# Logits and values from one matmul, and six groups of the result turned by VectorE instead of TensorE

## Chip, core and metric

The kernel runs on one NeuronCore of one Trainium2 chip. The metric is the time of one execution on the device in microseconds (us), as the median of several runs. The slots, groups and phases below are the kernel's own words for pieces of its schedule.

## What is computed

The input `z` has 4 batches of 1024 tokens with 128 features. It is normalised over the features (`xn`). One branch normalises again with a weight and a bias, projects to queries, keys and values of 16 heads with 8 features each, does softmax attention over 1024 keys per batch, projects back and adds `xn`. The other branch is a mixture of 8 experts, of which each token uses its two best. The two are multiplied and added to the input.

```python
xn = _layernorm(x)
zn = (z - mu) / jnp.sqrt(var + 1e-05) * ln_w + ln_b        # z is xn here
qkv = (zn @ W_qkv + b_qkv).reshape(b, n, 3, H, DH)
attn = jax.nn.softmax(einsum('bhqd,bhkd->bhqk', q, k) * scale)
s = xn + (attn @ v) @ W_proj + b_proj
logits = xf @ Wr + br                                      # xf is xn, 8 columns
# softmax over the two largest logits of each token
h = gelu(einsum('td,edh->eth', xf, W1) + b1)
g = silu(einsum('etd,te->td', einsum('eth,ehd->etd', h, W2) + b2, weights))
return x + s * g
```

## The kernel before, in words

The 4096 tokens are 8 groups (`g`) of 512. The kernel has an expert part and an attention part, and each engine's queue is written out by hand with numbered slots.

**Expert part.** Phase `g` has 32 slots for the experts of group `g`. In slot `i` TensorE does `up(i)` (three matmuls, L934 to L936) and `down(i - 3)` (L957, L958, L960, or L952). ScalarE does `gelu(i)` in slot `i` (L812 and L815, or L806). VectorE and GpSimd compute the low halves (`low_h`, L1239 and L670), VectorE also `combine` (L1256) in every fourth slot. The same slots hold the preparation of the next group, `pre(g + 1)`: transposes `t1` and `t2` (L882, L889), the router's logits (L897, 8 columns wide), queries and keys (`qk`, L906 and L907), the turned weights (`w_t`) and the values (`v`, L918: four matmuls of 128 columns). `run_slots` puts in each slot the step of `pre` ahead of that slot's expert step. On ScalarE `z_t` (L766) writes the normalised and turned `znT`, which `qk` and `v` read, and `tanh` (L791) feeds VectorE's `router_weights` (L1189 to L1194).

From slot 36 on, counted over all phases, the queues also hold the early row maxima of the attention scores: a score matmul on TensorE (L974) and a maximum on VectorE (L1321). They use two PSUM banks in turn, so the matmul of maximum `m` waits until maximum `m - 2` has been taken:

```python
EARLY_AT = [HT + 4 + (7 * m) // 10 for m in range(EARLY)]
...
                if m > 1:
                    pe.wait_ge(S("R"), m - 1)
```

That gives one or two of them in each slot. VectorE runs the maximum first in its slot, then the step of `pre`, then `low_h`. Queries and keys are split in three bf16 parts (`rest`, `second`, `third`), stored to DRAM by the SyncE queue, and read back as rows for the maxima (`sp_max_rows`, L433). The rows of head pair 0 need the parts of groups 0 and 1.

**Attention part.** 256 blocks of scores, exponentials (ScalarE, L855, two per block of about 1 us each) and products with the values (L1044). From block 243 on, TensorE's queue also holds the end of the first six groups, one step per block: `project(g)` (L1072) in one block and `y_turn(g)` (L1092, four transposes) in the next. VectorE adds and gates (`sum_y`, `gate_y`) and, after the turn, does `finish` (L1393), which adds the input held in `x_out`. Groups 6 and 7 follow behind the last block. The SyncE queue loads all of `x_out` at the start of the attention part (eight DMAs of 512-byte pieces) and stores it (L580) behind everything that it issues for the blocks.

Every wait of the kernel is on a semaphore with a constant count, in program order on each engine.

## Time and profile before

| | |
|---|---|
| median of 3 runs | 1032.16 us (1031.27 to 1032.86) |
| the profiled execution | 1031.52 us, span 1029.5 us |
| PE busy | 1008.1 us, 98% |
| DVE busy | 842.9 us, 82% |
| ACT busy | 859.4 us, 83% |
| POOL busy | 351.1 us, 34% |
| 16 DMA queues, share of packets | 26.5% |

The span is the part of the execution in which engines work, and what lies around it here is 2 us. The abbreviations: PE is TensorE, DVE VectorE, ACT ScalarE, POOL GpSimd, and SPq is the queue in which SyncE issues DMAs. Busy time of PE includes the pipelined stretch of a matmul, so neighbouring matmuls overlap in it and the distance of their starts is the better price.

### The profile page before, as it was taken

To read this page: it belongs to the slowest core of one execution; us is meant where nothing else is said; L and a number is where in the kernel's file an instruction comes from. 1 tells how busy PE (TensorE), PEld (TensorE's weight loads), DVE (VectorE), ACT (ScalarE), POOL (GpSimd) and SP (SyncE) were. 2 spreads that over 40 slices of the span, in tenths; PEclk is the share of its full clock that TensorE was granted. 3 is DMA by queue.
4 is the path that set the end of the run, shared out by engine and by line. 5 is a ranking of instruction groups with operands and counts; after the bars stand their busy time and mean duration, and the time that the engine had idled before them with its cause. 6 is when DMAs were issued, how large, how long until landed. Compare 5 with 4: busy or idle time off the path is not lost.

```text
span 1029.5 us, 17024 instructions
## 1 busy us (share of the span) xinstructions
PE 1008.1 (98%) x5837; PEld 443.0 (43%) x5869; DVE 842.9 (82%) x1283; ACT 859.4 (83%) x1166; POOL 351.1 (34%) x432
## 2 busy tenths in 40 slices
PE   6999999999999999999999999999999999999998
PEld 4676666666666666667222222222222222222222
DVE  5757878878887887785799999999999999999953
ACT  7877667676767767666999999999999999999985
POOL 5795665656575565746200010001000001000010
PEclk9999999999999999999999999999999999999999
DMA  6542322315132231412421222122221222212113
GB/s 198 131 117 60 103 56 59 102 32 145 31 93 69 57 118 33 113 39 69 116 53 50 55 60 57 42 60 54 54 63 43 58 53 53 59 51 57 26 26 88
DMA packets 102955, 72.11 MB, mean 70 GB/s; under 512 B 25737, under 2 KB 87878, under 8 KB 102870
## 3 DMA queue, kind: packets, MB, share of 16 engines
q1 hardware_dynamic: 102870, 71.04, 26.5%
q8 instruction: 46, 0.75, 0.3%
q14 instruction: 39, 0.32, 0.1%
HBM read 53.12 MB, written 15.59 MB: 67 GB/s over the span
## 4 chain that ended last, share of the span: by engine, by line
PE 87%; DVE 5%; issue 2%; ACT 2%; POOL 0%; another core or an unknown queue 0%; DVEq 0%; ACTq 0%; POOLq 0%
PE psum L1044 22%; PE psum L1004 13%; PE psum L989 10%; PE psum L974 6%; PE psum L934 5%; PE psum L936 5%; PE psum L935 5%; PE psum L952 5%; PE psum L960 4%; PE psum L957 4%; PE psum L958 4%; DVE neg_max_half L1321 1%; DVE neg_max_half L1295 1%; DVE neg_max_half L1291 1%; ACT p_ring L855 1%
## 5 line engine op out<-in xcount | busy, mean ns | idle before, releaser
L855 ACT ACTIVATE p_ring<-psum 128x1024 f32<-128x1024 f32 x512 | 494.5, 1031 | 19.6 <-PE psum L1004 9.1
L1291 DVE TENSOR_REDUCE neg_max_half<-psum 128x2 f32<-128x1024 f32 x240 | 294.3, 1226 | 42.3 <-PE psum L989 34.2
L1044 PE MATMUL psum<-p_ring,v_sb 128*9 128x512 f32 x2048 | 267.6, 594 | 0.2 <-ACT o_sb L846 0.2
L1321 DVE TENSOR_REDUCE neg_max_half<-psum 128x1 f32<-128x512 f32 x304 | 200.0, 685 | 74.9 <-PE psum L974 60.2
L812 ACT ACTIVATE h_hi<-psum,cols 128x512 fp32r<-128x512 f32 x192 | 132.4, 690 | 114.8 <-PE psum L936 114.0
L670 POOL TENSOR_TENSOR h_lo<-h_split,h_hi 128x512 fp32r<-128x512 f32 x128 | 166.2, 1300 | 151.8 <-ACT h_split L815 151.4
L1004 PE MATMUL psum<-q_stack,k_stack 51*128 51x512 bf16 x1024 | 201.2, 385 | 1.3 <-ACT p_ring L855 0.7
L989 PE MATMUL psum<-k_max_stack,q_max_stack 48*128 48x512 bf16 x720 | 182.2, 378 | 1.1
L1004 PEld LDWEIGHTS psum<-q_stack,k_stack 51*128 51x128 bf16 x1024 | 49.1, 92 | 296.6 <-ACT p_ring L855 282.7
L1295 DVE TENSOR_REDUCE neg_max_half<-psum 128x1 f32<-128x512 f32 x240 | 161.2, 672 | 0.0
L624 POOL CAST neg_max_parts<-neg_max_rest 128x16 bf16<-128x16 f32 x32 | 6.5, 203 | 448.4 <-DVE neg_max_rest L1304 448.2
L934 PE MATMUL psum<-xn_t_hi,w_lo 128*128 128x512 f32 x256 | 144.2, 563 | 0.4 <-ACT h_split L815 0.4
L815 ACT ACTIVATE h_split<-psum,cols 128x512 f32<-128x512 f32 x192 | 131.7, 686 | 0.0
L936 PE MATMUL psum<-xn_t_lo,w_hi 128*128 128x512 f32 x256 | 101.6, 397 | 0.0
L935 PE MATMUL psum<-xn_t_hi,w_hi 128*128 128x512 f32 x256 | 101.4, 396 | 0.0
L974 PE MATMUL psum<-k_max_stack,q_max_stack 128*128 128x512 bf16 x272 | 93.3, 385 | 2.6 <-DVE neg_max_half L1321 1.6
L960 PE MATMUL psum<-h_lo,w_hi 128*128 128x512 f32 x192 | 76.1, 396 | 2.2 <-POOL h_lo L670 1.4
L957 PE MATMUL psum<-h_hi,w_lo 128*128 128x512 f32 x192 | 75.7, 394 | 0.0
L958 PE MATMUL psum<-h_hi,w_hi 128*128 128x512 f32 x192 | 74.9, 390 | 0.0
L661 POOL TENSOR_TENSOR acc<-acc,prod 128x512 f32<-128x512 f32 x48 | 64.1, 1336 | 11.7 <-DVE prod L1256 11.7
L952 PE MATMUL psum<-h_full,w_full 128*128 128x512 f32 x128 | 65.4, 592 | 0.0
L1044 PEld LDWEIGHTS psum<-p_ring,v_sb 128*9 128x9 f32 x2048 | 31.3, 88 | 78.7 <-issue 76.4
(121 smaller groups left out, 967.9 us busy)
## 6 DMA issues: line engine op xcount, KB each, us to landing
expert_w_bc<-expert_w_dram SPq DMA_DIRECT2D x64, 256.0 KB, 4.9
k_rows_dram<-qk_parts SPq DMA_DIRECT2D x24, 256.0 KB, 2.8
q_max_stack<-q_rows_dram SPq DMA_DIRECT2D x64, 96.0 KB, 2.5
k_max_stack<-k_rows_dram SPq DMA_DIRECT2D x64, 96.0 KB, 2.5
q_stack<-q_rows_dram SPq DMA_DIRECT2D x64, 96.0 KB, 2.5
k_stack<-k_rows_dram SPq DMA_DIRECT2D x64, 96.0 KB, 2.5
q_rows_dram<-qk_parts SPq DMA_DIRECT2D x8, 384.0 KB, 2.6
xz<-in_L_attn_z_dram SPq DMA_DIRECT2D x8, 256.0 KB, 4.9
```

The source lines that it names most:

```text
L670: pool.tensor_tensor(hl[:, (g * HS + j) % HR, :], h32[:, (g * HS + j) % FR, :], hh[:, (g * HS + j) % HR, :].bitcast(F32), ALU.subtract)\
L855: act.activation(p_sb[:, n % PR, a, :, :].rearrange("p h t -> p (h t)"), scores_at(s), ACT.Exp, scale=SCALE).then_inc(S("P"), 1)
L934: pe.matmul(o, w1l[:, e, ws], G(xh, g), start=True, stop=False)
L935: pe.matmul(o, w1h[:, e, ws], G(xh, g), start=False, stop=False)
L936: pe.matmul(o, w1h[:, e, ws], G(xl, g), start=False, stop=True).then_inc(S("h"), 1)
L974: pe.matmul(early_bank[m % 2][:, :], q_m[:, p % 2, t * P:(t + 1) * P], k_m[:, p % 2, hh, c * TG:(c + 1) * TG], start=True, stop=True).then ...
L989: pe.matmul(max_bank(u)[:, :], q_m[rows, p % 2, t * P:(t + 1) * P], k_m[rows, p % 2, hh, c * TG:(c + 1) * TG], start=True, stop=True).then ...
L1004: i = pe.matmul(scores_at(s)[:, hh * TG:(hh + 1) * TG], k_s[rows, slot, kt * P:(kt + 1) * P], q_s[rows, slot, a * TG:(a + 1) * TG], start= ...
L1044: i = pe.matmul(o_bank[at:at + VR, :], v_sb[:, b * KT + kt, 2 * (p % PB) + hh, :], p_sb[:, n % PR, a, hh, :], start=(kt == 0), stop=(kt == ...
L1291: dve.tensor_reduce(flat[:, at[0]:at[1] + 1:at[1] - at[0]], psum[:, 5 * TG:7 * TG].rearrange("p (u t) -> p u t", u=2), AX.X, ALU.max, nega ...
L1295: dve.tensor_reduce(flat[:, at[0]:at[0] + 1], max_bank(units[0]), AX.X, ALU.max, negate=True).then_inc(S("R"), 1)
L1321: dve.tensor_reduce(mx[:, p % MXR, c, hh * NT + t:hh * NT + t + 1], early_bank[m % 2], AX.X, ALU.max, negate=True).then_inc(S("R"), 1)
```

## The change

Four things are done. In groups 1 to 7 the logits and the values come from one matmul of 136 columns with the unscaled `xnT` as stationary operand. For that, `ln_w` is multiplied into the value weights once (`value_weights`, ScalarE), the part of `ln_b` goes into the bias once (`value_bias`), and the second normalisation's factor is applied for each token when VectorE reads the result (`values_of`, four operations in place of one). The preparation of groups 1 to 7 gets other slots. Six groups of the result are turned by VectorE in blocks of 32x32, in SBUF, and `y_turn` leaves TensorE for them. And `x_out` of these six groups is loaded and stored in that blocked order: four DMAs of 64 KB each per group, in pieces of 128 bytes; the loads are spread over blocks 40 to 132. In the diff the slot tables (`return {...}`) come in the order GpSimd, ScalarE, TensorE, VectorE.

```diff
+        wvr_sb = fs("wvr_sb", [P, D + E])
+        wr_sb = wvr_sb[:, D:D + E]
...
+        lv_at = 5 * TG - (D + E)
+        lv = psum[:, lv_at:lv_at + TT * (D + E)].rearrange("p (t c) -> p t c", c=D + E)
...
-            for g in range(NG):
+            for g in range(BESIDE, NG):
                 sp.dma_start(x_out[:, g, :, :], x_g[g]).then_inc(S("tx"), 16)
+            x_at = {40 + 4 * k: k for k in range(BESIDE * P // TILE)}
...
+                if g < BESIDE:
+                    for a in range(P // TILE):
+                        sp.dma_start(out_tiles[g][:, :, a * TILE:(a + 1) * TILE], tile_rows(g, a))\
+                            .then_inc(S("out"), 16)
...
-                return {4: [rsqrt(g, 1)], 8: [rsqrt(g, 2)], 21: [rest(0)], 22: [rest(1)],
-                        25: [third(0)], 26: [third(1)]}
+                return {4: [rsqrt(g, 1)], 8: [rsqrt(g, 2)], 23: [rest(0)], 25: [rest(1)],
+                        27: [third(0)], 28: [third(1)]}
...
-                return {7: [normalise], 10: [x_t], 13: [z_scale], 15: [z_t], 17: [tanh], 19: [qk(0)], 21: [qk(1)], 23 if g else 27: [w_t]}
+                return {7: [normalise], 10: [x_t], 13: [z_scale], 18: [z_t, tanh], 21: [qk(0)], 23: [qk(1)], 25: [w_t]}
...
+                def logits_and_values():
+                    wait(pe, "xh", g, 1, 1)
+                    wait(pe, "kf", g, 1, 0)
...
+                    for t in range(TT):
+                        m = pe.matmul(lv[:, t, :], xnT[:, t * P:(t + 1) * P], wvr_sb[:, :], start=True, stop=True)
+                    m.then_inc(S("lg"), 1)
...
-                return {9: [t1], 12: [logits], 15: [t2], 18: [qk], 21 if g else 26: [w_t], 25: [v]}
+                return {9: [t1], 12: [logits_and_values], 17: [t2], 20: [qk], 23: [w_t]}
...
-                ends.setdefault(4 * g + 2, []).append(lambda g=g: y_turn(g))
...
+                        for t in range(t0, t1):
+                            i = dve.scalar_tensor_tensor(
+                                v_sb[:, g * TT + t, :, 0:DH], lv[:, t, 0:D].rearrange("p (h d) -> p h d", h=H),
+                                nwt[:, 4, t:t + 1], bv_bc[:, :].rearrange("p (h d) -> p h d", h=H), ALU.mult, ALU.add)
...
+                    return {0: [x_here, spread(0, 1)], 1: [spread(1, 4)], 3: [moments], 12: [low_x],
+                            14: [router_top], 15: [values_of(1, TT)],
+                            17: [router_weights], 18: [router_sum], 19: [router_done],
+                            26: [second(0)], 27: [second(1)]}
...
+            def turn_finish(g):
+                if g == 0:
+                    wait(dve, "tx", 0, 0, 16 * (NG - BESIDE + BESIDE * P // TILE))
+                wait(dve, "yg", 0, 0, g + 1)
+                dve.transpose(ffn[:, g, :], y[:, g, :]).then_inc(S("yt"), 1)
+                wait(dve, "yt", 0, 0, g + 1)
+                dst = x_out[:, g, :, :].rearrange("p t d -> p (t d)")
+                dve.scalar_tensor_tensor(dst, ffn[:, g, :], 0.5, dst, ALU.mult, ALU.add).then_inc(S("ty"), 1)
```

ScalarE's queue in slots 15 to 18 of phase 1, which prepares group 2. Before, the first pair of rows is slot 15 (`z_t`, `gelu(15)`):

```order
L766 ACTIVATE zn_t<-psum,cols 128x512
L806 ACTIVATE h_full<-psum,cols 128x512
L812 ACTIVATE h_hi<-psum,cols 128x512
L815 ACTIVATE h_split<-psum,cols 128x512
L791 ACTIVATE router<-router 128x32
L812 ACTIVATE h_hi<-psum,cols 128x512
L815 ACTIVATE h_split<-psum,cols 128x512
L812 ACTIVATE h_hi<-psum,cols 128x512
```

The same stretch in the changed kernel, whose line numbers are its own (L795 is `z_t`, L820 `tanh`):

```order
L841 ACTIVATE h_full<-psum,cols 128x512
L847 ACTIVATE h_hi<-psum,cols 128x512
L850 ACTIVATE h_split<-psum,cols 128x512
L847 ACTIVATE h_hi<-psum,cols 128x512
L850 ACTIVATE h_split<-psum,cols 128x512
L795 ACTIVATE zn_t<-psum,cols 128x512
L820 ACTIVATE router<-router 128x32
L847 ACTIVATE h_hi<-psum,cols 128x512
```

`z_t` moved behind three expert steps, and `tanh`, which stood ahead of `gelu(17)`, now stands behind it and behind `z_t`.

VectorE's queue in the same place of the changed kernel, slots 16 to 19 (L1403 are maxima, L1246 to L1251 `router_weights`, L1321 `low_h(16)`, L1255 to L1259 `router_sum`):

```order
L1403 TENSOR_REDUCE neg_max_half<-psum 128x1 x2
L1246 TENSOR_SCALAR router<-router 128x32
L1247 TENSOR_SCALAR router<-router 128x32
L1249 RECIPROCAL router<-router 128x32
L1251 TENSOR_TENSOR router<-router 128x32
L1321 TENSOR_TENSOR h_lo<-h_split,h_hi 128x512
L1403 TENSOR_REDUCE neg_max_half<-psum 128x1 x2
L1255 TENSOR_TENSOR router<-router 128x32
L1257 TENSOR_REDUCE router_sum<-router 128x4
L1259 RECIPROCAL router_sum<-router_sum 128x4
L1403 TENSOR_REDUCE neg_max_half<-psum 128x1
```

These rows stand in the order that they had before; what VectorE waits for at L1246 has moved on ScalarE.

GpSimd's queue in phase 0, in which group 1 is prepared, before (L610 is `third`):

```order
L610 TENSOR_TENSOR qk_parts<-qk_full,qk_parts 128x512
L670 TENSOR_TENSOR h_lo<-h_split,h_hi 128x512
L610 TENSOR_TENSOR qk_parts<-qk_full,qk_parts 128x512
L670 TENSOR_TENSOR h_lo<-h_split,h_hi 128x512
L661 TENSOR_TENSOR acc<-acc,prod 128x512
```

And in the changed kernel (L634 is `third`):

```order
L697 TENSOR_TENSOR h_lo<-h_split,h_hi 128x512 x2
L634 TENSOR_TENSOR qk_parts<-qk_full,qk_parts 128x512 x2
L688 TENSOR_TENSOR acc<-acc,prod 128x512
```

Both thirds now stand behind both low halves, so the stores of the queries too start later.

## Rows read from the trace of the kernel before

**Rows 1.** Windows: stretch, length, busy us of engines (instructions), clock, DMA share, GB/s.

```profile
86.00:486.00 400.00, 396.90 (x1663) 267.13 (x1694) 320.72 (x589) 276.42 (x477) 245.17 (x248) 1.00 0.28 73
496.00:984.00 488.00, 486.47 (x3605) 106.38 (x3605) 445.03 (x554) 474.03 (x512) 32.39 (x103) 1.00 0.22 57
984.00:1017.60 33.60, 33.43 (x213) 8.76 (x209) 13.29 (x21) 27.26 (x29) 5.14 (x5) 1.00 0.23 58
```

**Rows 2.** PE timeline around the logits of group 3: start, us, engine, line.

```profile
152.65 0.39 PE L958 MATMUL psum<-h_hi,w_hi 128*128 128x512 f32 x1
152.88 0.40 PE L960 MATMUL psum<-h_lo,w_hi 128*128 128x512 f32 x1
153.34 0.95 PE L897 MATMUL psum<-wr_sb,xn_t 128*128 128x8 f32 x8
...
154.47 0.39 PE L935 MATMUL psum<-xn_t_hi,w_hi 128*128 128x512 f32 x1
```

**Rows 3.** PE timeline around the values of group 3.

```profile
179.06 0.38 PE L974 MATMUL psum<-k_max_stack,q_max_stack 128*128 128x512 bf16 x1
...
180.40 0.40 PE L935 MATMUL psum<-xn_t_hi,w_hi 128*128 128x512 f32 x1
```

**Rows 4.** ACT timeline, slots 15 to 17 of phase 1.

```profile
99.16 0.78 ACT L766 ACTIVATE zn_t<-psum,cols 128x512 f32<-128x512 f32 x1 [0.41 <-PE psum L889]
...
102.63 0.23 ACT L791 ACTIVATE router<-router 128x32 f32<-128x32 f32 x1
103.08 0.69 ACT L812 ACTIVATE h_hi<-psum,cols 128x512 fp32r<-128x512 f32 x1 [0.23 <-PE psum L936]
103.67 0.68 ACT L815 ACTIVATE h_split<-psum,cols 128x512 f32<-128x512 f32 x1
```

**Rows 5.** DVE timeline, slots 17 to 19 of phase 1.

```profile
103.01 0.17 DVE L1189 TENSOR_SCALAR router<-router 128x32 f32<-128x32 f32 x1
...
104.40 1.28 DVE L1321 TENSOR_REDUCE neg_max_half<-psum 128x1 f32<-128x512 f32 x2
...
107.71 0.69 DVE L1321 TENSOR_REDUCE neg_max_half<-psum 128x1 f32<-128x512 f32 x1 [1.50 <-PE psum L974]
```

**Rows 6.** PE timeline, slots 18 and 19 of phase 1.

```profile
104.03 1.02 PE L906 MATMUL psum<-zn_t,wqkv_sb 128*128 128x512 f32 x2
...
106.44 1.02 PE L952 MATMUL psum<-h_full,w_full 128*128 128x512 f32 x2
107.30 0.38 PE L974 MATMUL psum<-k_max_stack,q_max_stack 128*128 128x512 bf16 x1
```

**Rows 7.** Timelines of POOL, SPq, PE, last third to first early score; page's DMA issues.

```profile
65.46 1.17 POOL L610 TENSOR_TENSOR qk_parts<-qk_full,qk_parts 128x512 bf16<-128x512 f32 x1
...
71.41 0.32 SPq L433 DMA_DIRECT2D q_max_stack<-q_rows_dram  x1
...
77.30 0.38 PE L974 MATMUL psum<-k_max_stack,q_max_stack 128*128 128x512 bf16 x1
...
q_max_stack<-q_rows_dram SPq DMA_DIRECT2D x64, 96.0 KB, 2.5
```

**Rows 8.** The chain that ended last, two blocks at the end: start, us, what.

```profile
999.53 1.05 PE psum L1072 x2
...
1002.23 0.66 PE psum L1092 x4
...
1004.51 1.05 PE psum L1072 x2
```

**Rows 9.** SPq timeline: the stores of the result.

```profile
1010.85 4.16 SPq L580 DMA_DIRECT2D out_dram<-x_out  x6
...
1025.87 1.22 SPq L580 DMA_DIRECT2D out_dram<-x_out  x2
```

**Rows 10.** DMA view, queue: packets, MB, share; windows 1010.8 to 1016.0, 1008.7 to 1010.19.

```profile
q1 hardware_dynamic: 2408, 1.25, 86.7%
...
q1 hardware_dynamic: 144, 0.01, 6.2%
```

More of the change, by code:

```diff
@@ L22 @@
 VC = 32
+TILE = 32
 EPS = 1e-5
@@ L83, in attention_and_experts @@
     out_g = out.rearrange("b (g t p) d -> (b g) p t d", p=P, t=TT)
+    x_tiles = x.rearrange("b (g c i) d -> (b g) i c d", i=TILE, c=TG // TILE)
+    out_tiles = out.rearrange("b (g c i) d -> (b g) i c d", i=TILE, c=TG // TILE)
     q_dram = nc.dram_tensor("q_rows_dram", (B, D, SLOTS, N), BF16, kind="Internal").ap()
@@ L764, in z_t @@
                     wait(act, "t2", g, 1, 1)
-                    wait(act, "v", g, 1, 0)
+                    if g == 1:
+                        act.wait_ge(S("v"), 1)
+                    wait(act, "k", g, 1, 0)
                     act.activation(znT[:, :], b6[:, :], ACT.Identity, scale=col(C_LNW), bias=col(C_LNB))\
@@ L796, in w_t, with value_weights @@
                     act.activation(wT, b5[0:TT * E, 0:P], ACT.Copy).then_inc(S("wT"), 1)
-                return {7: [normalise], 10: [x_t], 13: [z_scale], 15: [z_t], 17: [tanh], 19: [qk(0)], 21: [qk(1)], 23 if g else 27: [w_t]}
+                def value_weights():
+                    act.activation(wvr_sb[:, 0:D], wqkv_sb[:, 2 * D:3 * D], ACT.Copy, scale=col(C_LNW))\
+                        .then_inc(S("wv"), 1)
+                if g == 0:
+                    return {7: [normalise], 10: [x_t], 13: [z_scale], 15: [z_t], 17: [tanh], 19: [qk(0)], 21: [qk(1)],
+                            27: [w_t], 28: [value_weights]}
+                return {7: [normalise], 10: [x_t], 13: [z_scale], 18: [z_t, tanh], 21: [qk(0)], 23: [qk(1)], 25: [w_t]}
             def experts(g):
@@ L886, in t2 @@
                     wait(pe, "zn", g, 1, 1)
-                    wait(pe, "vd", g, 1, 0)
+                    if g:
+                        pe.wait_ge(S("vd_first"), g)
                     for t in range(TT):
@@ L903, in qk @@
                     wait(pe, "dlt", g, 1, 1)
+                    if g:
+                        pe.wait_ge(S("vd"), g + 1)
                     if g == 0:
@@ L920, in v @@
                     m.then_inc(S("v"), 1)
-                return {9: [t1], 12: [logits], 15: [t2], 18: [qk], 21 if g else 26: [w_t], 25: [v]}
+                if g == 0:
+                    return {9: [t1], 12: [logits], 15: [t2], 18: [qk], 26: [w_t], 25: [v], 27: [value_bias]}
+                return {9: [t1], 12: [logits_and_values], 17: [t2], 20: [qk], 23: [w_t]}
             def experts(g):
@@ L1227, in values, with values_of, step, value_bias @@
                                       .broadcast_to([P, TT, H, DH]), ALU.add).then_inc(S("vd"), 1)
+                def values_of(t0, t1):
+                    def step():
+                        if t0 == 0:
+                            wait(dve, "lg", g, 1, 1)
+                            wait(dve, "nwt", g, 2, 2)
+                            if g == 1:
+                                dve.wait_ge(S("bvn"), 1)
+                            if g == 2:
+                                dve.wait_ge(S("w_lo"), 2 * E)
+                        for t in range(t0, t1):
+                            i = dve.scalar_tensor_tensor(
+                                v_sb[:, g * TT + t, :, 0:DH], lv[:, t, 0:D].rearrange("p (h d) -> p h d", h=H),
+                                nwt[:, 4, t:t + 1], bv_bc[:, :].rearrange("p (h d) -> p h d", h=H), ALU.mult, ALU.add)
+                        i.then_inc(S("vd_first" if t0 == 0 else "vd"), 1)
+                    return step
+                def value_bias():
+                    dve.wait_ge(S("lnb_v"), 1)
+                    dve.wait_ge(S("vd"), 1)
+                    dve.tensor_tensor(bv_bc[:, :], b7[:, 0:D], bv_bc[:, :], ALU.add).then_inc(S("bvn"), 1)
+                if g:
+                    return {0: [x_here, spread(0, 1)], 1: [spread(1, 4)], 3: [moments], 12: [low_x],
+                            14: [router_top], 15: [values_of(1, TT)],
+                            17: [router_weights], 18: [router_sum], 19: [router_done],
+                            26: [second(0)], 27: [second(1)]}
                 return {7: [] if g else [normalise_rest], 0: [x_here, spread(0, 1)], 1: [spread(1, 4)], 3: [moments], 12: [low_x], 15: [router_top],
                         17: [router_weights], 18: [router_sum], 19: [router_done],
-                        24: [second(0)], 25: [second(1)], 28: [values]}
+                        24: [second(0)], 25: [second(1)], 28: [values], 29: [value_bias]}
             def experts(g):
@@ L1399, in _ @@
                 ends.setdefault(4 * g, []).append(lambda g=g: (sum_y(g), gate_y(g)))
-                ends.setdefault(4 * g + 2, []).append(lambda g=g: finish(g))
+                ends.setdefault(4 * g + 2, []).append(lambda g=g: turn_finish(g))
             dve.wait_ge(S("vd"), NG)
```

38 lines of the change are left out of this document (28 added, 10 removed).

## Prediction

> **What bounds the kernel now.** I read the windows by stage first, because the page's shares are averages over two very different parts. From 86 to 486 us (the expert phases after the first) TensorE is busy for 396.9 of 400 us, VectorE for 321 and ScalarE for 276: TensorE is the bound, and its queue has next to no gaps, so what is taken off it there comes back in full unless a new wait takes its place. From 496 to 984 us ScalarE is busy for 474 of 488 us and the exponentials set the pace; TensorE's 486 are the pipelined stretch of matmuls that wait for them. In the last blocks, 984 to 1017.6, it is TensorE again (33.4 of 33.6, ScalarE 27.3, VectorE 13.3) [rows 1]. So the change has three places to act: the slots of the preparation (TensorE bound, with VectorE in step through the row maxima), blocks 243 to 255, and the tail behind them, where SyncE's stores must land. Then I read the timelines of single slots, since every wait here is between neighbours in a hand-written order, and last the SyncE queue.
>
> **The price of the matmul that goes.** Undisturbed, two fp32r matmuls start 0.23 apart (L958, L960) [rows 2]. From the row-max matmul at 179.06 to L935 at 180.40 are 1.34 us, in which two such 0.23 lie; the four value matmuls take 0.88 [rows 3]. The logits by the same count take 1.59 - 0.46 = 1.13 with only 8 columns [rows 2], so the column count hardly sets the price and 136 columns are at most some 6% dearer than 128: I take 0.95 for the joint matmul, with 0.88 and 1.2 as bounds. Against the smaller reading (0.88 + 0.88) this saves 0.8 to 0.85 per group; 0.85 x 6 = 5.1 us in phases 1 to 6, and 0.85 in phase 0 (below). VectorE gets four operations of 128 columns for one of 512. Not shown in the trace; four such reads of PSUM cost between one 512-column read (0.6, half the pair in the row of maxima) and four of them (2.4) [rows 5]. VectorE has 79 us of idle time in these 400 [rows 1], and the reads stand in slots 14 and 15, ahead of a wait that is longer (next term), so I count nothing.
>
> **The wait that the new slots make.** In phase 1 `tanh` runs at 102.63, ahead of `gelu(17)` at 103.08, and VectorE's L1189 starts 0.38 behind it, at 103.01 [rows 4, 5]. In the changed order `tanh` stands behind both operations of `gelu(17)` (0.59 and 0.57) and behind `z_t` (0.78 long, about 0.7 to the next start). `gelu(17)` itself is released by TensorE at 103.08 and can't come earlier. So `tanh` starts at about 103.08 + 1.16 + 0.7 = 104.94, and VectorE's L1189 at 105.3 instead of 103.01: it stands 2.3 us in the queue's slot 17. Queued behind it are `low_h(16)` and the two maxima of slot 18, which start 1.39 behind L1189 (103.01 to 104.40) and take 0.6 each [rows 5]: the first is done at 105.3 + 1.4 + 0.6 = 107.3. TensorE may issue the row-max matmul of slot 19 only then. It stood at 107.30 before, but behind `qk`, which took 1.72 (104.03 to 106.44, less three matmuls of 0.23) [rows 6] and now stands two slots later, behind it. Without a wait the matmul would come at 107.30 - 1.72 = 105.6. So TensorE waits 1.7 us there, and then still has `qk` to do. What was hidden was that VectorE had 1.50 us of idle time just there, given by `qk` [rows 5]; that cover has moved away from the place that needs it. The pattern of one or two maxima per slot repeats every seven slots. By it phases 1, 2, 3, 5 and 6 meet the same wait in slot 19 and phase 4 in slot 20, where I count 1.4. Sum 5 x 1.7 + 1.4 = +9.9 us. Bounds: nothing, if VectorE's queue makes the time up before TensorE asks; and 2.3 a phase (the whole delay), +13.8.
>
> **Phase 0** (prepares group 1; ScalarE and TensorE share the bound, no maxima yet). `low_h(16)` is late here too; `down(16)` waits for it, `qk` comes after: about +1, bounds 0 and 1.7. Further on, the last `third` ends at 66.63, the rows of head pair 0 are asked for at 71.41 and the first early matmul runs at 77.30 [rows 7]. Four loads, issued some 0.5 apart as near as SyncE's other rows show, of which the last lands 2.5 behind its issue, make 75.4, so almost 2 us are to spare [rows 7, 9]. Now the last `third` stands behind one more `low_h` (1.3) and the three stores of the queries start only one `third` ahead of those of the keys (+0.5), and slots 27 and 28 for 25 and 26 add some 0.7: the rows land 2.5 later, at 78 or so, while TensorE, 0.85 sooner, is there at 76.4. The saving of this phase is lost and +0.5 on top. Phase 0 together: +1.5, bounds 0 and +3. The new one-off operations (`value_weights`, `value_bias`) are three small ones, taken to lie inside this.
>
> **Blocks 243 to 255.** One `project` to the next is 4.98 us (999.53 to 1004.51), with `y_turn` 0.66 of them on TensorE's chain [rows 8]. Without it a pair of blocks is 4.31 of TensorE against four exponentials, which are 3.7 to 4.0 of ScalarE (474 us over 512 operations before, or 488 with their gaps) [rows 1]: TensorE stays the bound, so 0.66 comes back for each of six, 4.0; the last block ends on an exponential, so I take -3.8 (bounds -2.5 and -4.0). VectorE's blocked transpose of 128x512 is not in the trace; between one 0.6 pass over 512 columns and a few of them it fits, since VectorE is idle for 20 of these 33.6 us [rows 1], and nobody but the stores waits for it.
>
> **The stores.** SyncE starts them at 1010.85, behind the blocks' own DMAs; six of 256 KB take 4.16 us to issue, and that of group 6 goes out at 1025.87 [rows 9]. The start hangs on the copy of the last-but-one pair's sums in block 249 and moves by three turns, to 1008.9; group 6 moves by 3.8, to 1022.1. In these 13.2 us now 24 stores must be issued instead of 6, 0.55 each; six took 0.69 each, with the DMA queues full. A 512-byte packet costs 0.867 x 16 x 5.2 / 2408 = 30.0 ns of a queue, a 64-byte packet 0.062 x 16 x 1.49 / 144 = 10.3 ns [rows 10]. 128 bytes lie between; nearest is the 64-byte row, I take 16 ns: 32 packets x 16 = 0.51 us per store and queue, 12.3 for all, just inside. I count +0.5 for it (bounds 0 and, at 30 ns, 23 us: the queues would be done at 1032 and groups 6 and 7 some 8 us late). The loads of `x_out` move from the part's start, where nothing waited, to 24 issues in 92 blocks, of some 0.5 us each: nothing.
>
> The Trainium skill speaks against this part: "DMA: Bandwidth & Descriptors", Specifications, gives 512 bytes as the least for line rate and a read-modify-write below. The 64-byte row above shows no such cost, but it is a short burst. By that rule the estimate would be a packet as dear as one of 512 bytes, which is the third rival.
>
> **Sum.** -5.1 (values) + 9.9 (slot 17) + 1.5 (phase 0) - 3.8 (turns) + 0.5 (stores) = +3.0 on the profiled execution's 1031.5 us: 1034.5. That execution lies 0.6 under the median of the runs, so the median comes to about 1035.
>
> **Rivals.**
> 1. The wait in slot 17 doesn't reach TensorE, since VectorE catches up in its idle time. For it: 79 us of idle in 400. Against: none of that is between slot 17 and slot 19 once `qk` has left. It gives 1035 - 9.9 - 1 = 1024, faster.
> 2. The forecast's waits, and the head pair's rows are later still or `low_h` slows under GpSimd's load (the upper bounds, 13.8 and 3): 1040.
> 3. A 128-byte store costs as much as a 512-byte one, from about 18 ns on the stores decide the end: with the waits 1035 + 7.5 = 1042; without them 1032.
>
> **How the numbers follow.** Forecast 0.48 (its own range 1031 to 1038), rival 1 0.30, rival 2 0.10, rival 3 0.12. About 0.2% (2.1 us, 1030.1 to 1034.2) is what can be told from no change. Faster: nearly all of rival 1 (0.27) and the lowest of the forecast (0.03), 0.30. Same: 0.17 of the forecast, 0.03 of rival 1, 0.20. Slower: 0.28, 0.10 and 0.12, 0.50. The range that leaves out no more than 2 in 10 takes in rival 1 almost wholly and the foot of rival 3: 1023 to 1042.
>
> **What would show it.** Right: VectorE's `router_weights` with an idle time of about 2 us ahead of it, released by ScalarE's `tanh`, in seven groups; TensorE's row-max matmul of slot 19 with a wait of 1.5 to 2 us for VectorE in phases 1 to 6, 10 us in all; the distance from one group's joint matmul to the next about 0.9 longer than that of the logits before; a gap ahead of the first early matmul; `project` to `project` 4.3 us. Wrong: no wait of TensorE on VectorE in these slots (rival 1); the last store issued later than 4 us behind its `finish`, or packets of over 18 ns (rival 3). A joint matmul of more than 1.2 us would take back the saving.

## Result and the profile after

The changed kernel takes 1053.74 us (median of 4 runs, 1052.87 to 1055.08) against 1031.78 of the kernel before (4 runs): ratio 1.0207, interval 1.0190 to 1.0223, so 22 us slower. The forecast was 1035.0 with a range of 1023 to 1042. The profiled execution has a span of 1053.3 us (before 1029.5).

The windows of the changed kernel come first: stretch, length, then busy time of PE, PEld, DVE, ACT and POOL, the granted clock, DMA share and GB/s. They run from the joint matmul of group 2 to the first score matmul, from there to the first `project`, and over the ends.

```profile
95.25:517.94 422.69, 400.86 (x1607) 264.73 (x1636) 327.23 (x602) 274.24 (x474) 248.80 (x249) 0.98 0.26 69
517.94:1011.87 493.93, 490.96 (x3628) 107.99 (x3627) 447.32 (x556) 479.73 (x517) 35.22 (x106) 1.00 0.23 56
1011.87:1045.00 33.13, 32.34 (x200) 8.26 (x199) 17.99 (x30) 28.48 (x31) 4.75 (x4) 1.00 0.24 38
```

The same first stretch of the kernel before, logits of group 2 to the first score:

```profile
92.24:490.36 398.12, 395.30 (x1654) 266.01 (x1682) 317.74 (x584) 275.47 (x474) 244.91 (x249) 1.00 0.28 73
```

Here lies the loss: 422.69 against 398.12, +24.6. TensorE is busy 5.6 us longer for less work, and its clock shows 0.98 for 1.00: it ran part of its matmuls at half speed. It also has 21.8 us of idle time for 2.8. Ahead of this stretch 3.0 are lost (95.25 against 92.24), the middle costs nothing, and the ends give 3.5 back.

Then the waits of the changed kernel (engine, what it would write, its line, who let it go: us in total, times, longest), the two that matter:

```profile
PE psum L1030 <- DVE neg_max_half L1403: 19.1, 22, 2.0
DVE router L1246 <- ACT router L820: 18.7, 8, 3.0
```

So the predicted wait is there, VectorE behind `tanh` and TensorE's row-max matmul behind VectorE. But TensorE's waits of this kind add up to 19.1 us for the forecast's 10, since others have come beside that of slot 19. Phase 1 in the changed kernel, VectorE in slots 14 and 17 (start us, us, engine, line):

```profile
100.78 0.36 DVE L1235 MAX8 top<-logits 128x8 f32<-128x8 f32 x4
101.17 0.87 DVE L1238 TENSOR_TENSOR router<-logits,top 128x32 f32<-128x32 f32 x1
101.97 1.32 DVE L1240 TENSOR_TENSOR router<-logits,top 128x32 f32<-128x32 f32 x1
...
109.21 0.58 DVE L1246 TENSOR_SCALAR router<-router 128x32 f32<-128x32 f32 x1 [2.09 <-ACT router L820]
...
110.40 0.69 DVE L1321 TENSOR_TENSOR h_lo<-h_split,h_hi 128x512 fp32r<-128x512 f32 x1
111.00 1.28 DVE L1403 TENSOR_REDUCE neg_max_half<-psum 128x1 f32<-128x512 f32 x2
```

GpSimd at the same time:

```profile
100.72 2.52 POOL L697 TENSOR_TENSOR h_lo<-h_split,h_hi 128x512 fp32r<-128x512 f32 x2 [3.80 <-ACT h_split L850]
...
108.47 1.28 POOL L697 TENSOR_TENSOR h_lo<-h_split,h_hi 128x512 fp32r<-128x512 f32 x1 [1.19 <-ACT h_split L850]
```

And TensorE:

```profile
103.95 0.39 PE L1030 MATMUL psum<-k_max_stack,q_max_stack 128*128 128x512 bf16 x1 [0.80 <-DVE neg_max_half L1403]
...
108.75 1.02 PE L1006 MATMUL psum<-h_full,w_full 128*128 128x512 f32 x2
111.75 0.39 PE L1030 MATMUL psum<-k_max_stack,q_max_stack 128*128 128x512 bf16 x1 [1.98 <-DVE neg_max_half L1403]
...
114.51 1.91 PE L958 MATMUL psum<-zn_t,wqkv_sb 128*128 128x512 f32 x2
```

The last two operations of `router_top`, over 32 columns, are a subtraction (L1238) and a comparison (L1240). They took 0.19 and 0.18 in this phase of the kernel before, where they started behind GpSimd's pair:

```profile
100.34 0.19 DVE L1181 TENSOR_TENSOR router<-logits,top 128x32 f32<-128x32 f32 x1
100.45 0.18 DVE L1183 TENSOR_TENSOR router<-logits,top 128x32 f32<-128x32 f32 x1
```

```profile
97.67 2.52 POOL L670 TENSOR_TENSOR h_lo<-h_split,h_hi 128x512 fp32r<-128x512 f32 x2 [3.76 <-ACT h_split L815]
```

Now they take 0.87 and 1.32. The second ends at 103.29, and GpSimd's pair of `low_h` at 100.72 + 2.52 = 103.24. `MAX8`, just ahead of them and beside the same GpSimd operation, is not held. The first operation of `router_weights` took 0.17 [rows 5]; now it takes 0.58 and ends at 109.79, GpSimd's `low_h(17)` at 109.75. And `q`'s matmul pair takes 1.91 for 1.02 [rows 6]. The windows of the changed kernel just behind the wait show why:

```profile
112.00:113.00 1.00, 1.00 (x6) 0.82 (x5) 0.93 (x5) 0.12 (x1) 0.21 (x1) 1.00 0.00 0
113.00:114.00 1.00, 1.00 (x4) 0.28 (x3) 1.00 (x3) 0.56 (x1) 0.00 (x0) 0.52 0.00 0
114.00:115.00 1.00, 1.00 (x3) 0.67 (x2) 0.83 (x3) 0.00 (x0) 0.77 (x1) 0.50 0.02 8
115.00:116.00 1.00, 1.00 (x2) 0.34 (x1) 0.62 (x2) 0.00 (x0) 0.50 (x1) 0.50 0.24 68
116.00:117.00 1.00, 1.00 (x4) 0.50 (x2) 0.00 (x0) 0.00 (x0) 0.00 (x0) 0.78 0.35 82
117.00:118.00 1.00, 1.00 (x5) 0.68 (x4) 0.00 (x0) 0.00 (x0) 0.00 (x0) 1.00 0.67 123
```

The granted clock (third number from the right) goes from 1.00 to 0.50, that is from 2.4 to 1.2 GHz, and back. The work missed is the sum of what each stretch lacks to 1: 0.48 + 0.50 + 0.50 + 0.22 = 1.7 us. There are five such falls in this profile, in phases 1, 2, 3, 5 and 6, each behind a wait of 1.95 to 1.98; by the same sum over all of them they cost 8.5 us. Behind the wait of 1.12 in phase 4 there is none.

The ends: in the changed kernel the chain that ended last has `project` 4.25 after `project` (start us, us, what), where it was 4.98 [rows 8], and SyncE's stores:

```profile
1011.94 1.05 PE psum L1128 x2
1016.19 1.05 PE psum L1128 x2
```

```profile
1035.60 13.90 SPq L601 DMA_DIRECT2D out_dram<-x_out  x24
1049.59 1.23 SPq L604 DMA_DIRECT2D out_dram<-x_out  x2
```

From 1036 to 1048, with only these stores running, the DMA view has 10182 packets in a share of 69.8% of 16 engines: 0.698 x 16 x 12 / 10182 = 13.2 ns per 128-byte packet.

```profile
q1 hardware_dynamic: 10182, 1.30, 69.8%
```

### The profile page after: what moved, and what is told of

The parts are those of the page before. It is cut to its first block, busy times and chain, and to the rows that moved or that the text cites. A ratio compares the mean times of both kernels' runs of the same rounds, so it can differ in the third digit from the quotient of the medians.

```text
span 1053.3 us, 16943 instructions
## 1 busy us (share of the span) xinstructions
PE 1008.8 (96%) x5759; PEld 438.3 (42%) x5791; DVE 853.4 (81%) x1311; ACT 857.6 (81%) x1167; POOL 355.5 (34%) x432
## 4 chain that ended last, share of the span: by engine, by line
PE 78%; DVE 10%; issue 4%; ACT 3%; POOL 1%; DMA 1%; SPq 0%; DVEq 0%; ACTq 0%; another core or an unknown queue 0%; POOLq 0%
PE psum L1100 21%; PE psum L1060 13%; PE psum L1045 10%; PE psum L1030 5%; PE psum L988 4%; PE psum L990 4%; PE psum L989 4%; PE psum L1006 4%; PE psum L1014 3%; PE psum L1011 3%; PE psum L1012 3%; DVE neg_max_half L1403 3%; DVE neg_max_half L1377 1%; DVE neg_max_half L1373 1%; ACT p_ring L890 1%
## 5 line engine op out<-in xcount | busy, mean ns | idle before, releaser
L1403 DVE TENSOR_REDUCE neg_max_half<-psum 128x1 f32<-128x512 f32 x304 | 199.1, 683 | 75.9 <-PE psum L1030 60.1
L697 POOL TENSOR_TENSOR h_lo<-h_split,h_hi 128x512 fp32r<-128x512 f32 x128 | 168.5, 1322 | 158.8 <-ACT h_split L850 158.5
L1030 PE MATMUL psum<-k_max_stack,q_max_stack 128*128 128x512 bf16 x272 | 96.9, 392 | 20.7 <-DVE neg_max_half L1403 19.1
L841 ACT ACTIVATE h_full<-psum,cols 128x512 f32<-128x512 f32 x64 | 44.4, 694 | 29.9 <-PE psum L990 29.9
```

Source lines behind the costliest of these rows:

```text
L697: pool.tensor_tensor(hl[:, (g * HS + j) % HR, :], h32[:, (g * HS + j) % FR, :], hh[:, (g * HS + j) % HR, :].bitcast(F32), ALU.subtract)\
L1030: pe.matmul(early_bank[m % 2][:, :], q_m[:, p % 2, t * P:(t + 1) * P], k_m[:, p % 2, hh, c * TG:(c + 1) * TG], start=True, stop=True).then ...
L1403: dve.tensor_reduce(mx[:, p % MXR, c, hh * NT + t:hh * NT + t + 1], early_bank[m % 2], AX.X, ALU.max, negate=True).then_inc(S("R"), 1)
```

## Experiments

Each experiment shows its edit, cut where `...` stands. The theories. **A:** the whole loss is the wait behind `tanh` and the clock that falls behind it. **B:** the new joint matmul or the reads of the values are dearer than counted. Later **A2** was added: in slot 14 `router_top` meets GpSimd's `low_h` pair and stands still beside it. Each run's "before" is the kernel before on the same chip.

**The ends alone**, on the kernel before.

```
-            for g in range(NG):
+            for g in range(BESIDE, NG):
                 sp.dma_start(x_out[:, g, :, :], x_g[g]).then_inc(S("tx"), 16)
...
-                ends.setdefault(4 * g + 2, []).append(lambda g=g: y_turn(g))
...
-                ends.setdefault(4 * g + 2, []).append(lambda g=g: finish(g))
+                ends.setdefault(4 * g + 2, []).append(lambda g=g: turn_finish(g))
...
```

> The kernel before with only the other half of the change: VectorE turns the gated sums of six groups, x and the result go by 128-byte packets, TensorE's four transposes a group go. Theory A: project to project 4.25 for 4.98, so -3.6 us, 1028.2. Rival (the loads or the stores of 128 bytes take some of it back): -2 or less, with the last packets of the stores later against the last finish than before.

Measured: 1027.60 against 1031.48, -3.9 by the medians, ratio 0.9952 (0.9940 to 0.9965). This half does what was forecast, and the stores cost nothing that can be seen.

**The other half alone:** the same lines taken back out of the changed kernel.

> The changed kernel with the ends of the kernel before (TensorE's transposes of y, 512-byte rows of x and result): only the half of the change that concerns the expert phases. If the halves don't touch each other, the time is 1053.7 + 3.9 = 1057.6; if the 128-byte loads or stores disturb or help anything else, it lies more than 1.5 us off that.

Measured: 1051.64 (1049.88 to 1056.59), not 1057.6. The profile, of the run at 1049.88, has the same five waits of 1.96 but two falls of the clock instead of five. Three falls are 5.1 us. The four runs lie 6.7 us apart, in the order of their mean clocks: 0.996, 0.996, 0.993 and 0.991 for 1049.88, 1050.64, 1052.64 and 1056.59. So the times alone are too noisy to say whether the halves add up. The profiles say more. The first score matmul comes at 509.18 for 517.94, 8.8 sooner, of which three falls are 5.1 and the start of the program 0.5 (first joint matmul at 37.29 for 37.83). The other 3.1 lie in phases 3, 4 and 6 (1.1, 1.1 and 1.0, without the falls). These are the phases in which the comparison of `router_top` takes 0.18 here and 1.32 in the changed kernel; the runs below show what holds it. With that and the falls taken into account, the halves add up.

**`tanh` back in slot 17**, in the changed kernel.

```
-                return {7: [normalise], 10: [x_t], 13: [z_scale], 18: [z_t, tanh], 21: [qk(0)], 23: [qk(1)], 25: [w_t]}
+                return {7: [normalise], 10: [x_t], 13: [z_scale], 17: [tanh], 18: [z_t], 21: [qk(0)], 23: [qk(1)], 25: [w_t]}
```

> The changed kernel with ScalarE's tanh in slot 17, ahead of gelu(17), and z_t alone in slot 18. Theory A (the wait behind tanh, and the clock that falls after it, are the whole loss): VectorE's router_weights start about 2 us sooner, TensorE's 19 us of waits in slot 19 go to under 3, its granted clock stays at 1.00 there, and the time falls by 5 to 6 phases of 4 us: 1053.7 becomes about 1025 to 1030, below the kernel before. Rival B (the joint matmul, or the four reads of PSUM by VectorE, are dearer than thought): the time stays within 3 us of 1053.7. Rival C (z_t, now first behind gelu(17), was part of it and qk has to be in its old place as cover): half comes back, about 1040.

Measured: 1031.59 against 1031.48, ratio 0.9995 (0.9987 to 1.0004). 22 us come back, the 2 us waits are gone and the clock falls nowhere. `tanh`'s place is most of the loss, and B is out as its main cause. But the time is 1.6 above the top of the range expected and 4.0 above the kernel with the ends alone, and with the saved matmuls it should lie below that. What is left in this kernel's TensorE timeline is one wait of 0.79 to 0.86 in phases 1, 2, 5 and 6:

```profile
102.12 0.39 PE L1030 MATMUL psum<-k_max_stack,q_max_stack 128*128 128x512 bf16 x1 [0.80 <-DVE neg_max_half L1403]
```

**`router_top` back in slot 15 as well.**

```
-                            14: [router_top], 15: [values_of(1, TT)],
+                            15: [router_top], 16: [values_of(1, TT)],
```

> The changed kernel with tanh in slot 17 and, in addition, VectorE's router_top back in slot 15 and the three later value operations in slot 16. Theory A2 (in slot 14 the two subtractions of router_top stand still while GpSimd's low_h pair runs, 0.87 and 1.32 for 0.19 and 0.18, and TensorE's row-max matmul then waits 0.8 in each of phases 1 to 6): the subtractions take 0.2 to 0.5 again, the 0.8 waits go, and the time falls from 1031.6 by 4 to 5 us, to about 1027. Rival (the 0.8 is the four value operations that VectorE has more of): TensorE still waits 0.5 or more a phase and the time stays within 1.5 us of 1031.6.

Measured: 1025.89 against 1031.42, ratio 0.9944 (0.9932 to 0.9957): the fastest kernel here. The two operations of VectorE are short again, and they start after GpSimd's pair has ended (99.19 + 2.52 = 101.71):

```profile
102.01 0.19 DVE L1238 TENSOR_TENSOR router<-logits,top 128x32 f32<-128x32 f32 x1
102.12 0.18 DVE L1240 TENSOR_TENSOR router<-logits,top 128x32 f32<-128x32 f32 x1
```

```profile
99.19 2.52 POOL L697 TENSOR_TENSOR h_lo<-h_split,h_hi 128x512 fp32r<-128x512 f32 x2 [3.79 <-ACT h_split L850]
```

The value operations are as many as before this edit, only a slot later. That fits theory A2, but their move was part of the edit, so the next run takes them out of the question.

**`router_top` in slot 14, on the kernel before**, which has no value operations there.

```
-                return {7: [] if g else [normalise_rest], 0: [x_here, spread(0, 1)], 1: [spread(1, 4)], 3: [moments], 12: [low_x], 15: [router_top],
+                return {7: [] if g else [normalise_rest], 0: [x_here, spread(0, 1)], 1: [spread(1, 4)], 3: [moments], 12: [low_x], 14 if g else 15: [router_top],
```

> The kernel before with VectorE's router_top in slot 14 for 15 in the groups after the first, nothing else. Theory A2: its two subtractions run beside GpSimd's low_h pair and take about 0.9 and 1.3 together in most phases, ending where GpSimd's operation ends; VectorE is 1.6 to 2 us later, TensorE waits 0.3 to 0.8 a phase, and the time grows by 1 to 5 us. Rival (the long subtractions come from the new reads of values): they keep 0.2 to 0.5 and the time does not change.

Measured: 1034.32 against 1031.42, +2.9 by the medians, ratio 1.0024 (1.0016 to 1.0033). VectorE and GpSimd of this kernel:

```profile
97.87 1.01 DVE L1181 TENSOR_TENSOR router<-logits,top 128x32 f32<-128x32 f32 x1
98.80 1.32 DVE L1183 TENSOR_TENSOR router<-logits,top 128x32 f32<-128x32 f32 x1
```

```profile
97.56 2.52 POOL L670 TENSOR_TENSOR h_lo<-h_split,h_hi 128x512 fp32r<-128x512 f32 x2 [3.77 <-ACT h_split L815]
```

98.80 + 1.32 = 100.12, and 97.56 + 2.52 = 100.08. The slot alone makes the two operations long; the second takes 1.32 to 1.34 in each of phases 1 to 6. The Trainium skill ("SBUF — State Buffer", SBUF: two separate sides) says that VectorE and GpSimd share a pair of ports as an exclusive lock, which a VectorE operation with two inputs in SBUF, or one in a two-port mode, needs while GpSimd works, and that the loser stands still until the other's whole instruction is done. The trace agrees: both operations have two SBUF inputs and the second ends 0.04 to 0.05 behind GpSimd's pair.

The two traces of the changed kernel itself show it too. GpSimd's pair is two instructions, and between them VectorE's second operation can slip in. In the first trace it was held in all six phases (1.32 each). In the second it slipped in once, in phase 1, and there TensorE's wait of 0.80 at 103.95 is absent:

```profile
102.11 0.87 DVE L1238 TENSOR_TENSOR router<-logits,top 128x32 f32<-128x32 f32 x1
102.90 0.18 DVE L1240 TENSOR_TENSOR router<-logits,top 128x32 f32<-128x32 f32 x1
```

With `tanh` back in slot 17 it was held in phases 1, 2, 5 and 6 only. In phase 3 the versions of the changed kernel in which it is held have a wait of 1.20, and those in which it slips in lack it. So two runs of one kernel can differ by this too.

**`router_top` in slot 15, `tanh` left in slot 18.**

> The changed kernel with router_top back in slot 15 and the later values in slot 16, tanh left in slot 18. Theory A2 with A: the 0.8 waits go, the 2 us waits behind tanh and the clock that falls after them stay: 1053.7 - 4.5 = 1049. If the waits behind tanh take up what is gained (VectorE then only waits longer), the time stays within 2 us of 1053.7.

Measured: 1040.95 (1040.20 to 1042.21), not 1049. The 0.8 waits are gone, five of 1.96 stay, and the clock falls once in the profile, costing 1.7. Against the kernel with both put back, the first score comes at 503.47 instead of 488.17: 15.3 later, 13.6 without the fall. That is the price of `tanh`'s place with the clock taken out. The waits behind it make 10.9 of this, and 0.9 lies in phase 0 (94.58 for 93.72 at the joint matmul of group 2); the other 1.8 were not taken apart. Against the changed kernel the first score comes 14.5 sooner: 6.8 are four falls, 0.8 the start of the program, and 6.8 are left for `router_top`'s slot with its operation held in six phases. That is 1.1 a phase; with `tanh` in slot 17 it was 4.8 for four phases, 1.2 each.

**`tanh` in slot 18, on the kernel before**, where `qk` still covers VectorE.

```
-                return {7: [normalise], 10: [x_t], 13: [z_scale], 15: [z_t], 17: [tanh], 19: [qk(0)], 21: [qk(1)], 23 if g else 27: [w_t]}
+                return {7: [normalise], 10: [x_t], 13: [z_scale], 15: [z_t], 18 if g else 17: [tanh], 19: [qk(0)], 21: [qk(1)], 23 if g else 27: [w_t]}
```

> The kernel before with tanh moved behind gelu(17), to slot 18, in the groups after the first, and nothing else; qk stays in slot 18 of TensorE. Theory A (qk in slot 18 covers the delay of VectorE): router_weights start 1.2 to 2 us later, but TensorE waits less than 0.5 us a phase and the time grows by 0 to 3 us. Rival (tanh's place alone makes the loss, cover or no cover): TensorE waits 1.2 us or more a phase, the clock falls, and the time grows by 10 to 20 us.

Measured: 1037.25 against 1031.48, ratio 1.0045 (1.0030 to 1.0060). By the interval that is 3 to 6 us slower, between what the two theories expected. The largest waits of TensorE here are 0.57 to 0.69, in three phases, and the clock doesn't fall. So `qk` covers most of it but not all. VectorE's operation behind `tanh` is long here too, with GpSimd's beside it, though it has only one SBUF input (no row shows in which mode it runs):

```profile
104.48 1.23 DVE L1189 TENSOR_SCALAR router<-router 128x32 f32<-128x32 f32 x1 [1.41 <-ACT router L791]
```

```profile
104.41 1.26 POOL L670 TENSOR_TENSOR h_lo<-h_split,h_hi 128x512 fp32r<-128x512 f32 x1 [1.77 <-ACT h_split L815]
```

It ends at 105.71, GpSimd's at 105.67. That raised the question whether `tanh` or GpSimd sets the end of the wait.

**`tanh` ahead of `z_t`**, both still in slot 18 of the changed kernel: `18: [tanh, z_t]` for `18: [z_t, tanh]`.

> The changed kernel with tanh and z_t in slot 18 the other way round: tanh still behind gelu(17), but ahead of z_t. Theory A: VectorE starts router_weights 0.6 to 0.7 sooner, TensorE's waits in slot 19 go from 1.97 to 1.3 (1.12 to 0.5 in phase 4). What this run is for: whether the clock still falls after 1.3 us of idleness. If it doesn't (as in phase 4 after 1.12), the time is 1053.7 - 4.5 (waits) - 8.5 (clock) = 1041; if it still falls in most phases, 1049.

Measured: 1051.77 (1048.65 to 1056.26); the waits did not become shorter. VectorE, GpSimd and TensorE of this kernel:

```profile
107.91 1.24 DVE L1246 TENSOR_SCALAR router<-router 128x32 f32<-128x32 f32 x1 [1.42 <-ACT router L820]
```

```profile
107.84 1.28 POOL L697 TENSOR_TENSOR h_lo<-h_split,h_hi 128x512 fp32r<-128x512 f32 x1 [1.19 <-ACT h_split L850]
```

```profile
111.11 0.39 PE L1030 MATMUL psum<-k_max_stack,q_max_stack 128*128 128x512 bf16 x1 [1.98 <-DVE neg_max_half L1403]
```

Against GpSimd's start VectorE begins 0.07 later instead of 0.74, and the operation takes 1.24 instead of 0.58: it ends 1.31 and 1.32 behind that start, the same. So theory A's step that VectorE goes on when `tanh` ends fails. What ends the wait is `low_h(17)` on GpSimd, which starts when `gelu(17)` is done. The clock fell behind all six waits in the profiled run, the 1.12 of phase 4 too.

**`low_h(16)` and `low_h(17)` exchanged between VectorE and GpSimd**, on top of that. The semaphore counts that others wait for are changed with it.

```
         def by_vector(i):
-            return i % HC == 0
+            return i == 4 * HC + 1 if i // HC == 4 else i % HC == 0
...
```

> The changed kernel with tanh ahead of z_t in slot 18 (as in the run before, where that alone moved nothing), and low_h(16) and low_h(17) exchanged between VectorE and GpSimd, in all groups. GpSimd then runs nothing when VectorE comes to router_weights behind gelu(17); VectorE has one pass of 0.6 less in slot 17 and one more in slot 18. If GpSimd's operation is what held router_weights (it took 1.24 and ended with GpSimd's), that operation takes 0.3 or less, tanh's 0.66 come through, and TensorE's waits in slot 19 go from 1.97 to 0.1 to 0.7; the clock falls in none or few phases, and the time comes to 1032 to 1042. If tanh itself sets the end, the wait only loses the pass that left slot 17, so 1.3 a phase, and the time is 1043 to 1050.

Measured: 1041.15 (1039.72 to 1041.26), clock 0.999 in the profile. VectorE's operation is short, 0.18 in all seven groups, and GpSimd is idle beside it:

```profile
106.99 0.18 DVE L1246 TENSOR_SCALAR router<-router 128x32 f32<-128x32 f32 x1 [1.43 <-ACT router L820]
...
108.99 1.22 DVE L1255 TENSOR_TENSOR router<-router 128x32 f32<-128x32 f32 x1
```

```profile
105.69 1.28 POOL L697 TENSOR_TENSOR h_lo<-h_split,h_hi 128x512 fp32r<-128x512 f32 x1
108.86 1.30 POOL L697 TENSOR_TENSOR h_lo<-h_split,h_hi 128x512 fp32r<-128x512 f32 x1 [1.88 <-ACT h_split L850]
```

```profile
108.53 0.39 PE L1030 MATMUL psum<-k_max_stack,q_max_stack 128*128 128x512 bf16 x1 [0.30 <-DVE neg_max_half L1403]
...
111.89 0.39 PE L1030 MATMUL psum<-k_max_stack,q_max_stack 128*128 128x512 bf16 x1 [1.34 <-DVE neg_max_half L1403]
```

The exchange did what GpSimd's part in it says: TensorE's wait of 1.98 is 0.30. Of the 1.68 between them 0.6 is VectorE's own `low_h`, which has left this slot, and 1.06 the operation behind `tanh`, 0.18 for 1.24. But new waits come a slot on. In phase 1 the router's next operation meets `low_h(18)` (1.22 long, ending at 110.21 with GpSimd's at 110.16), and TensorE waits 1.34; phase 5 is alike, with 1.35. In phases 3, 4 and 6, with waits of 1.06, 1.52 and 1.05, it is VectorE's own `low_h` that is long beside GpSimd's, 1.78 for 0.69:

```profile
233.89 1.78 DVE L1321 TENSOR_TENSOR h_lo<-h_split,h_hi 128x512 fp32r<-128x512 f32 x1
```

**Work in the idle time:** two more 128x512 matmuls in slot 18 of the changed kernel, their result unused.

```
+                def fill():
+                    pe.wait_ge(S("vd"), g + 1)
+                    for _ in range(2):
+                        pe.matmul(b5[:, :], wqkv_sb[:, 0:D], wqkv_sb[:, 0:D].unsqueeze(1).broadcast_to([P, TT, D]), start=True, stop=True)
...
-                return {9: [t1], 12: [logits_and_values], 17: [t2], 20: [qk], 23: [w_t]}
+                return {9: [t1], 12: [logits_and_values], 17: [t2], 18: [fill], 20: [qk], 23: [w_t]}
```

> The changed kernel with two more matmuls of 128x512 (the size of qk, 1.7 us the pair) on TensorE in slot 18 of each preparation after the first; their result is not used. Theory A (about half of the loss of a phase is the clock that falls to half after the 2 us of idleness): the added work stands in the idle time, the granted clock stays at 1.00, L958 goes back from 1.91 to 1.02, and the time falls by about 1.9 us in each of 5 or 6 phases: 1053.7 - 10 = 1044. Rival (the clock falls for another cause, or the time behind the wait is lost elsewhere): work is added and nothing comes back, so 1053.7 to 1064.

Measured: 1048.54 (1047.52 to 1051.52). Adding 1.7 us of matmul to each phase makes the kernel 5 us faster by the medians, and the intervals of the two ratios don't touch (1.0144 to 1.0185 here, 1.0190 to 1.0223 for the changed kernel). The clock is 1.00 throughout and `q`'s pair takes 1.02:

```profile
112.00:117.00 5.00, 4.32 (x16) 2.49 (x16) 3.89 (x8) 0.79 (x2) 2.21 (x2) 1.00 0.09 21
```

```profile
114.06 0.39 PE L1035 MATMUL psum<-k_max_stack,q_max_stack 128*128 128x512 bf16 x1 [0.68 <-DVE neg_max_half L1408]
114.28 1.02 PE L958 MATMUL psum<-zn_t,wqkv_sb 128*128 128x512 f32 x2
```

It gained 5 and not 10. The expectation took 1.9 for a fall where one costs 1.7, 8.5 for five. Between the two profiled runs the gain is 7.6, of which 1.0 is the start of the program (36.81 for 37.83). In phases 1 and 5 a later router operation now stands still beside GpSimd (L1260, 1.17 and 1.18 long), and TensorE waits 0.68 and 0.70 for what is behind it. What else takes up the difference was not taken apart.

**The changed kernel once more.**

> The changed kernel once more, for a second profile. In the first the granted clock fell after five of six waits of about 1.97 us; in kernels that differ elsewhere it fell after two or one of five waits as long. If this depends on chance or on a moment outside the program, the number of falls differs here too and the phases with and without one differ by 1.7 to 1.9 us; if it is fixed by the program, the same five phases show it.

Measured: 1052.14 in its one run, three falls of the clock (phases 3, 5 and 6), 5.1 us. In phase 1 TensorE has the same wait, and the clock stays:

```profile
111.72 0.39 PE L1030 MATMUL psum<-k_max_stack,q_max_stack 128*128 128x512 bf16 x1 [1.96 <-DVE neg_max_half L1403]
```

```profile
113.00:114.00 1.00, 1.00 (x6) 0.62 (x5) 1.00 (x3) 0.54 (x1) 0.00 (x0) 1.00 0.00 0
114.00:115.00 1.00, 1.00 (x3) 0.38 (x2) 1.00 (x3) 0.00 (x0) 0.79 (x1) 1.00 0.03 8
```

**All small steps near their old slots:** `t2` and `z_t` 16, `qk` 18, its parts 19 and 21, `w_t` 21 on TensorE and 23 on ScalarE, GpSimd's steps 21, 22, 25 and 26, VectorE's `second` 24 and 25, on top of the fastest version.

> A version meant to beat both: the changed kernel's work (joint matmul, values from it, turned ends) with the small steps of the groups after the first put back near their old slots: t2 and z_t 16, tanh 17, qk 18, qk parts 19 and 21, the transpose of the weights 21, GpSimd's rest 21 and 22 and third 25 and 26, VectorE's second 24 and 25, router_top 15, values 15 and 16. By theory: phases 1 to 6 as in the run with router_top in slot 15 (60.0 to 60.9 each), and in phase 0 the 1.45 us lost there against the kernel before come back, as GpSimd's third no longer stands ahead of its low_h in slots 27 and 28: about 1024.5. Rival (what phase 0 loses comes from the new one-off operations): 1026 again, and more if qk now waits for the values of slot 16.

Measured: 1026.83 against 1031.22, ratio 0.9963 (0.9949 to 0.9976), no better than 1025.89. Phase 0 is 56.70 long as before the edit (56.71), against 55.26 in the kernel with the ends alone. So the 1.45 lost there do not come from these slots; TensorE's waits in it just move, from GpSimd's `low_h` (1.8) to that (1.1) and to the values (0.7). What in phase 0 costs them stays open. The first score matmul comes 1.3 later than in the fastest version, nearly all of it in phase 3, where TensorE has a new wait of 1.25.

## Why the prediction was wrong, step by step

The starts of the first score matmul, which leave the ends out, give the parts: 490.31 with the ends alone, 517.94 in the profiled run of the changed kernel.

| part | forecast | measured | from |
|---|---|---|---|
| values saved, phases 1 to 6 | -5.1 | -3.8 | both slots put back against ends alone, without phase 0 |
| phase 0 | +1.5 | +1.7 | the same two, up to 92.05 and 93.72 |
| `router_top` in slot 14 | 0 | +4.8 | 488.17 to 493.00 |
| `tanh` in slot 18, without the clock | +9.9 | +13.6 | 488.17 to 503.47, less one fall |
| falls of the clock | not counted | +8.5 | five in the profiled run |
| start of the program | not counted | +0.8 | group 1's joint matmul at 37.83, for 37.01 in the fastest version |
| `router_top`, held in phases 3 and 4 too | 0 | +2.0 | rest to 517.94 |
| ends and stores | -3.3 | -3.9 | ends alone, by its time |

**What bounds the kernel** was read rightly, TensorE with VectorE in step through the row maxima.

**The values** were sized a little high. By the forecast's own prices 0.88 + 0.88 - 0.95 is 0.81 a group, 4.9 and not 5.1. The joint matmul takes 0.97 to 1.09, the forecast's 0.95 nearly, but phase 4 gives nothing back, with a wait of 0.86 in it. This is also what the change is worth when its steps stand well: 1025.89 against 1027.60.

**The wait in slot 17** was found where it is, and its size at TensorE was right: 1.98, 1.96, 1.97, 1.12, 1.96 and 1.95 make 10.9 for 9.9. Its cause was half right. `tanh` does stand behind `gelu(17)`, but what holds VectorE to the end is GpSimd's `low_h(17)`, released by the same `gelu(17)`: with `tanh` 0.66 sooner the wait is still 1.98, and with GpSimd idle the operation behind `tanh` takes 0.18 for 1.24. The forecast added up 1.16 + 0.7 of ScalarE and came near the true figure by accident; the step "so `tanh` starts at 104.94, and L1189 at 105.3" doesn't decide, as the run with `tanh` ahead of `z_t` shows. The sign that joint matmuls would stand 0.9 further apart than the logits did is missed by far: 64.66 for 61.10 in phase 1.

**The first step that failed** is "I count nothing" for VectorE in slots 14 and 15, since it "has 79 us of idle time". That weighed the four value reads, which are cheap, 0.34 and 0.85 for three. It didn't ask what `router_top` meets a slot earlier. The trace of before had the answer: in phase 1 GpSimd's `low_h` pair ran from 97.67 to 100.19, and the two short operations started at 100.34. In phase 2 the first was already held: it took 0.48 and ended at 161.35, GpSimd's pair at 161.30. Moved a slot ahead both lie beside it. The runs showed 4.8 us for this with the second operation held in four phases, and about 2 more with it held in six.

**The second** is "Sum", which prices an idle microsecond of TensorE as one. Behind a wait of 2 us the clock may fall, and each fall costs 1.7 more; the upper bound of 13.8 left that out. The 4.8 and 2.0 of `router_top`, the 8.5 of the clock, 3.7 more for `tanh`'s place and 0.8 at the start make 19.8 of the 20.7 us that lie between the forecast's sum (+3.0) and the table's (+23.7). The 2.0 is a rest, but it has the size that two phases cost in the other profiles (1.0 to 1.2 each). Of the 3.7, 0.9 lies in phase 0, where the forecast had booked it.

**Phase 0** came out near the forecast in size, and half for its reasons. In the changed kernel it is 57.42 long, 2.2 more than before, where the forecast had 1.5. 0.9 comes with `tanh`'s place, as forecast (+1), and TensorE waits 0.31 for the rows of head pair 0. But 1.45 is also lost in the fastest version, where `tanh` stands in its old slot, and for that the forecast has no reason.

**The ends** were right: 4.25 from `project` to `project` for the forecast's 4.3, and -3.9 for -3.8.

**The stores** cost less than taken, 13.2 ns per 128-byte packet for 16, where a 512-byte one costs 30.0 [rows 10]. The store of group 6 goes out at 1049.59, right behind its `finish` (1048.88 + 0.68). The third rival is out. "DMA: Bandwidth & Descriptors" (Specifications) of the Trainium skill, cited in the forecast, gives 512 bytes as the least for line rate and a read-modify-write below. The first fits: by the byte these packets are 1.8 times as dear (4 x 13.2 = 53 for 30.0). The forecast's estimate from the second, a packet as dear as one of 512 bytes, does not hold in this stretch.

**The rivals:** the first, no wait at TensorE, is contradicted by the 10.9 us of waits in the place that it names. The second, later by up to its bounds, names neither `router_top`'s slot nor the clock.

## What to carry to other kernels

When a small operation of VectorE is moved, look at what GpSimd runs at its new time: an operation over 32 columns took as long as what was left of GpSimd's 128x512 operation, 1.3 for 0.2, and so did one with a single SBUF input (1.24 for 0.17). Idle time of VectorE elsewhere does not pay for it. Price a new wait of a bound TensorE at more than its length where it may drop the clock, and test it by putting unused matmuls into the gap. And when an edit moves the step that covers another engine's lateness, put the slots back one by one: the same work was 1053.7 or 1025.9 us by the slots of three small steps.

## Not expected of the hardware

The granted clock fell behind some waits of TensorE and not behind others of the same length at the same place. Behind the waits of 1.95 to 1.98 it fell five times in five and three times in five in two profiles of the changed kernel, twice in five without the turned ends, once in five with `router_top` in slot 15. Behind a wait of 1.12 it fell in one profile (phase 4 of the run with `tanh` ahead of `z_t`, where it fell behind all five long ones too), and not in the others. The run times follow it: of that kernel the four runs are 1056.26, 1052.93, 1050.62 and 1048.65 us at mean clocks of 0.988, 0.993, 0.993 and 0.996. In the profiles whose longest wait of this kind lay between 0.86 and 1.52 (`tanh` back in slot 17, `router_top` back as well, all steps near their old slots, the exchange, the added matmuls) no fall was seen. The Trainium skill ("TensorE: Matmul & The Clock Gate", What's actually happening) says that the chip lowers the clock by how busy it sees TensorE; the rows agree that idleness comes first. Two runs of the changed kernel, with five falls and three, show that the program alone doesn't fix it. What decides between two equal waits is open.
